# Macaron block on one core (MoE, windowed top-k attention, MoE): the POOL pauses removed and the five interleaving tables replaced

## What is computed

```
x = x + 0.5 * ffn(layernorm(x))
x = x + attn(layernorm(x))
x = x + 0.5 * ffn(layernorm(x))

ffn(x):  n = layernorm(x) * ln_gamma + ln_beta
         gates = softmax over the two largest of softmax(n @ router_w.T)      # 8 experts
         sum over the 2 chosen experts e of gate_e * (silu(n@Wg_e.T) * (n@Wu_e.T)) @ Wd_e.T     # width 384
         + a shared expert of width 128 for every token
attn(x): windows of 128 tokens; q, k, v = x@W.T + b; scores / sqrt(128);
         only the 32 largest scores of each row are kept; softmax; @ v; leaky relu; + x; layernorm * gamma + beta
```

## Time and profile before

| | us |
|---|---|
| median of 3 runs | 647.05 |
| lowest, highest | 643.54, 648.61 |
| the profiled execution | 641.43 |
| its span (first to last instruction) | 639.5 |
| PE busy | 517.6 (81%) |
| POOL busy | 441.3 (69%) |
| DVE busy | 391.3 (61%) |
| ACT busy | 341.0 (53%) |
| mean granted TensorE clock | 0.936 |

### The profile page before, as it was taken

One profiled execution on the slowest core, in us unless ns is written; L12 is line 12 of the kernel. 1 busy time (PEld: TensorE's weight loads), 2 busy tenths in 40 slices (PEclk: granted clock), 3 DMA queues, 4 the chain that ended last, 5 costly groups with the idle time before them and its releaser, 6 DMA issues.

```text
span 639.5 us, 15747 instructions
## 1 busy us (share of the span) xinstructions
PE 517.6 (81%) x3928; PEld 468.7 (73%) x3928; DVE 391.3 (61%) x1785; ACT 341.0 (53%) x816; POOL 441.3 (69%) x806
## 2 busy tenths in 40 slices
PE   2957899779879998987896359887598987999882
PEld 2646797769879898877694348775588977999871
DVE  5586765532255886985797758888567452222454
ACT  3444455364435877745766158673564574455340
POOL 1566878888877457577288815888688888766453
PEclk9995999999989999999899569998799999999897
DMA  6915746566576454764221453531455665676894
GB/s 190 317 45 173 223 164 206 182 211 230 201 256 245 166 191 146 252 215 156 96 88 43 128 175 108 178 113 42 142 196 189 226 213 208 220 282 225 273 316 141
DMA packets 88021, 117.89 MB, mean 184 GB/s; under 512 B 11848, under 2 KB 60880, under 8 KB 87936
## 3 DMA queue, kind: packets, MB, share of 16 engines
q1 hardware_dynamic: 76208, 96.75, 44.8%
q0 software_dynamic: 9312, 19.16, 8.6%
q10 hardware_dynamic: 2416, 0.99, 0.7%
HBM read 26.57 MB, written 26.19 MB: 82 GB/s over the span
## 4 chain that ended last, share of the span: by engine, by line
PE 44%; issue 14%; POOL 12%; DMA 8%; DVE 8%; ACT 7%; SPq 4%; another core or an unknown queue 3%; ACTq 0%; POOLq 0%; DVEq 0%
PE ps_y L732 10%; PE ps_g L718 9%; POOL results L1578 5%; PE ps_h L723 5%; PE ps_u L723 4%; POOL rows L1549 3%; POOL still L1535 3%; DMA xin<-rows 2%; DMA raw_dn<-in_dnw 2%; PE ps_x L712 2%; DVE xres L1308 2%; PE w L676 2%; PE w L630 2%; PE w L660 2%
## 5 line engine op out<-in xcount | busy, mean ns | idle before, releaser
L1578 POOL DMA_INDIRECT results<-raw_gu,idx x163 | 162.5, 997 | 93.4 <-ACT raw_gu L941 50.3
L732 PE MATMUL ps_y<-dn_t,raw_gu 128*128 x978 | 142.5, 283 | 23.4 <-issue 11.1
L1549 POOL DMA_INDIRECT rows<-zz,s_idx x128 | 129.5, 1012 | 32.2 <-issue 17.4
L732 PEld LDWEIGHTS ps_y<-dn_t,raw_gu 128*128 128x128 f32 x978 | 124.3, 194 | 33.3 <-issue 32.6
L718 PE MATMUL ps_g<-x_t,raw_dn 128*128 128x128 f32 x978 | 140.5, 281 | 0.0
L718 PEld LDWEIGHTS ps_g<-x_t,raw_dn 128*128 128x128 f32 x978 | 126.3, 197 | 3.2 <-issue 3.2
L941 ACT COPY raw_gu<-ps_y 128x128 f32<-128x128 f32 x163 | 43.0, 264 | 122.1 <-PE ps_y L732 79.3
L935 ACT ACTIVATE sil<-ps_g 128x384 f32<-128x384 f32 x163 | 80.1, 491 | 48.6 <-PE ps_g L718 30.5
L931 ACT ACTIVATE x_t<-ps_x,bf_c,gf_c 128x128 f32<-128x128 f32 x163 | 75.5, 463 | 44.0 <-PE ps_x L712 32.7
L1381 DVE TENSOR_TENSOR raw_gu<-sil,ps_h 128x384 f32<-128x384 f32 x81 | 44.6, 551 | 82.1 <-PE ps_h L723 33.0
L1535 POOL IOTA still<- 128x200 int32 x291 | 90.7, 312 | 5.6
(11 more groups left out here) (167 smaller groups left out, 761.4 us busy)
## 6 DMA issues: line engine op xcount, KB each, us to landing
raw_dn<-gu_t SPq DMA_DIRECT2D x163, 384.0 KB
xin<-rows SPq DMA_DIRECT2D x163, 64.5 KB
yg<-results SPq DMA_DIRECT2D x15, 512.0 KB
results<-raw_gu,idx POOLq DMA_INDIRECT x163
rows<-pads SPq DMA_DIRECT2D x40, 64.5 KB
rows<-pads SPq DMA_DIRECT2D x5, 451.5 KB
rows<-zz,s_idx POOLq DMA_INDIRECT x128
out<-xres SPq DMA_DIRECT2D x7, 256.0 KB
```

The lines of the kernel that those rows point to most:

```text
L732: t = pe.matmul(ps_y[:, 0, :], h_t[:, k4, c * P:(c + 1) * P], dn[:, bass.ds(off + c * D, D)], start=(c == 0), stop=(c == FC - 1))
L1549: pool.indirect_dma_start(xs, bass.IndirectOffsetOnAxis(s_idx[n][:, c, k:k + 1], 0), zz[n][:, k, c, :], None).then_inc(scat[n], 16)
L1578: pool.indirect_dma_start(yt, bass.IndirectOffsetOnAxis(idx[:, ky:ky + 1], 0), yb[:, ky, :], None).then_inc(yst[ky], 16)
```

## The change

The iota, its tile `still`, its semaphore `rested` and both calls of `apart_in_time` are gone. The five lists of `WEAVE` are replaced: the number of calls of `turn()` and the parts are the same (660 on PE, 497 on ACT, 171 on DVE, 326 on POOL and on SP), their places differ.

```diff
 WEAVE = {
     "sp": """
-        8 3 2 14 2 2 8 5 35 z1 8 50 z1 7 26 z2 58 5 10 2 4 60 4 2 z1 6 z1 2 z1 3 z6""",
+        9 1 17 1 15 z1 8 4 20 12 5 44 3 19 12 z1 33 26 5 2 9 26 38 z1 7 z2 3 z1 2 5 z6""",
...
     "pool": """
-        z20 1 1 z2 1 z1 1 z2 2 2 z2 4 z1 2 z1 2 z1 3 2 z1 1 z1 2 z1 2 1 1 2 z1 2 2 2 2 z1 4 4 4 4 4 3 5 z1 2 4 4 4 2 2 z1 28 18 6 z1 4 z1 4 z1 2 2 z1 6 8 z1 2
-        2 z2 2 1 z2 1 z8 6 4 z1 2 2 2 z2 2 2 z1 6 z1 2 2 1 z5 1 z2 1 5 z1 2 4 2 z1 8 z1 2 2 4 2 z1 1 5 z3 2 6 3 5 z1 4 4""",
+        z19 1 z5 2 z2 5 z1 3 z2 1 z1 5 z1 2 z1 3 1 z3 2 9 4 2 z1 2 2 z2 17 20 z1 3 z2 2 z1 2 1 5 2 2 8 z3 3 3 24 z1 3 1 4 z2 1 z1 8 3 1 3 z4 3 z1 4
+        3 z9 6 z1 8 z1 1 1 z1 2 z2 1 z1 1 z1 2 z3 2 3 5 1 5 z3 2 z1 1 5 2 2 6 z2 2 z2 5 z1 2 13 z2 8 13 3 4 1 23""",
 }
...
-        still = sb("still", [P, 2, 200], I32)
...
-        out_st, spare, rested = sem("out_st"), sem("spare"), sem("rested")
+        out_st, spare = sem("out_st"), sem("spare")
...
-            rests = itertools.count()
-
-            def apart_in_time():
-
-                n = next(rests)
-                if n >= 2:
-                    pool.wait_ge(rested, n - 1)
-                pool.iota(still[:, n % 2, :], pattern=[[1, 200]], base=0, channel_multiplier=0).then_inc(rested, 1)
-
...
                         pool.indirect_dma_start(xs, bass.IndirectOffsetOnAxis(s_idx[n][:, c, k:k + 1], 0),
                                                 zz[n][:, k, c, :], None).then_inc(scat[n], 16)
-                        apart_in_time()
                         turn()
...
                     pool.indirect_dma_start(yt, bass.IndirectOffsetOnAxis(idx[:, ky:ky + 1], 0),
                                             yb[:, ky, :], None).then_inc(yst[ky], 16)
-                    apart_in_time()
```

More of the change, by code:

```diff
@@ L121 @@
+        9 z3 1 2 6 z2 8 z3 2 2 z3 3 3 z2 1 1 z3 2 z1 1 z2 4 z2 1 z1 2 z3 5 z1 1 8 z1 1 z2 1 z4 1 z2 2 1 z21 1 1 1 4 z3 2 z3 4 2 2 7 1 2 z7 1 2 z1 2
+        z4 1 z3 2 3 1 3 1 1 z1 2 z5 1 z2 1 z1 4 3 6 z3 3 z1 7 z3 2 11 3 z2 3 z1 5 50 46 43""",
     "dve": """
-        z51 1 z3 1 z1 1 z6 1 z14 1 z7 1 z2 1 z1 1 z68 2 z9 1 z7 1 z13 1 z9 1 z4 1 z1 1 z10 1 z14 1 z13 2 z4 1 z1 1 z10 1 z10 1 z4 1 z1 1 z5 1 z2 18 z3 1 z5 1
-        z4 1 z7 1 z11 1 1 z1 1 z3 1 z2 1 z3 1 z9 1 z8 1 z11 1 z4 1 z4 1 z3 1 z3 1 z3 1 z7 1 z13 1 1 1 z4 1 z4 1 z7 1 z6 1 z3 1 z9 1 z17 1 z12 1 z3 1 1 z5 1
@@ L124 @@
-        z12 1 z3 1 z3 1 z1 1 z6 1 z5 1 z8 1 z13 1 z28 1 z3 1 z4 1 z5 1 z7 1 z7 1 1 z89 2 z9 1 z32 1 z3 1 z4 1 z4 1 z8 1 z3 1 z4 1 z13 1 z40 1 1 1 z5 1 z6 1
-        z46 1 z17 1 z2 1 z4 1 z10 1 z2 1 1 z23 1 z1 1 z19 1 1 z2 1 z14 4 z25 1 z16 2 z5 2 z2 30 z7 2 z7 2 z7 3 z7 2 z7 1 z7 1 z8""",
+        z68 1 z10 2 z2 1 z3 1 z21 1 z14 1 1 z38 2 z12 2 z11 1 z1 1 z14 1 z1 1 z3 1 z14 1 z8 1 z9 1 z2 2 z3 2 2 z4 1 z3 1 z16 1 1 z3 1 z1 4 3 1 z3 5
+        z9 1 z9 1 z6 3 z7 1 1 z1 1 z10 1 z2 1 z1 1 z14 1 1 z12 1 z7 1 z2 1 z2 1 z2 1 z5 1 z14 1 z5 1 2 z12 1 z3 2 z9 1 z9 1 z1 1 z18 1 z2 1 z8 1 1
@@ L126 @@
+        z4 1 z14 1 z8 2 z15 2 z9 1 z14 2 z28 1 z3 1 z8 1 1 z5 1 z6 1 z10 1 z97 1 z3 1 z3 1 z20 1 z3 1 z9 2 z5 1 z4 1 z19 2 z37 1 z2 1 z12 1 z20 1 1
+        z22 1 z19 1 z2 1 z10 2 z14 2 z16 1 z4 1 1 z6 1 z29 4 z24 1 z2 1 z5 3 z1 4 2 6 z5 1 z1 8 z2 4 z1 2 z2 2 1 z2 2 z5 1 z8 1 z4 1 z3 1 z1 1 1 z2
+        2 z6 2 z15""",
     "pool": """
-        z20 1 1 z2 1 z1 1 z2 2 2 z2 4 z1 2 z1 2 z1 3 2 z1 1 z1 2 z1 2 1 1 2 z1 2 2 2 2 z1 4 4 4 4 4 3 5 z1 2 4 4 4 2 2 z1 28 18 6 z1 4 z1 4 z1 2 2 z1 6 8 z1 2
-        2 z2 2 1 z2 1 z8 6 4 z1 2 2 2 z2 2 2 z1 6 z1 2 2 1 z5 1 z2 1 5 z1 2 4 2 z1 8 z1 2 2 4 2 z1 1 5 z3 2 6 3 5 z1 4 4""",
+        z19 1 z5 2 z2 5 z1 3 z2 1 z1 5 z1 2 z1 3 1 z3 2 9 4 2 z1 2 2 z2 17 20 z1 3 z2 2 z1 2 1 5 2 2 8 z3 3 3 24 z1 3 1 4 z2 1 z1 8 3 1 3 z4 3 z1 4
```

8 lines of the change are left out of this document (3 added, 5 removed).

## The result

The changed kernel takes 711.85 us in the median of 4 runs (711.27 to 715.83), the kernel before 645.29 us (642.73 to 648.61) on the same chip: the ratio is 1.1054, 95% interval 1.1001 to 1.1108. The forecast was 622 us, within 606 to 642. It was wrong in its sign. The profiled execution took 711.72 us, its span 709.8 us at a mean granted clock of 0.886 (before: 639.5 at 0.936).

The account below looks back on a forecast made before the run. The prediction took PE as the main bound, with POOL saturated in two stretches and making PE wait for rows. Terms 8.3 + 6 + 4.5 + 5.9 = 24.7 us off 641.43 gave 616.7, by the ratio 622 us; range 606 to 642.

Parts of the forecast that it names:

- POOL's time: Sign for the whole run: POOL busy near 350 us once the iotas are gone.
- The SP queue's waits behind POOL's number copies: Sign: the SP queue's 68.7 us of waiting for POOL's copies of result numbers falls by half.
- Block 62 and block 148: Sign against the forecast: a new PE wait for rows there would mean step 6's or 15's moved scatters come too late.
- b): Passage between the layers: POOL's scatters finish earlier, so PE's wait for rows shortens; 6 us gained.
- c): Second such wait, at 454 us: POOL's scatter of step 12 comes earlier; 4.5 us gained, bounds 2 and 5.8.
- the slower rival: Back-to-back indirect DMAs hold each other up with 1.49 us records; by the ratio 675 us, chance 0.09.
- What a pause costs: Pricing step over 291 DMAs: 0.25 us saved with a copy between, 0.41 without, 93 us of POOL's time.
- The pitch: Sign: POOL's indirect DMAs follow at 1.00 to 1.16 us, or 1.35 with a copy between.
- a): 64 to 192 us: with POOL freed, PE goes from 86% to 95% busy; 8.3 us gained, bounds 3 to 14.
- d): 480 to 544 us: POOL's time falls by 12 us and PE reaches 95%; 5.9 us gained, bounds 2 and 6.6.
- e): The rest: the new lists alone, at unchanged speeds, are worth 0, with -8 to +8 us.
- The pause covered something: Rival: POOL's descriptor makers stay busy past the DMA record, so pitch stays 1.48; by the ratio 645 us, chance 0.10.

Follow-up runs that it names:

- e2: The changed kernel (new lists) with the pauses put back; 650.11 us, ratio 1.0003 to the kernel before.
- m4: Separate kernel computing nothing of the layers: six phases of back-to-back indirect DMAs beside one engine pair, the last two ACT to DVE and DVE to ACT; latest signal 17.47 us.
- e1: The kernel before with its old lists and the pauses taken out; 675.04 us, ratio 1.0452.
- m2: Separate kernel, layers left out: TensorE streams matmuls beside POOL's DMAs; a round takes 5.02 us with indirect DMAs without pauses, 2.01 with pauses of 480 elements.

## Why the prediction was wrong

**What held.** POOL's time: 353.4 us for about 350. The lists at zero: e2 has 1.0003. The SP queue's waits behind POOL's number copies fell from 68.7 us to half, as said, in the queue's own waits of the kernel after:

```profile
SPq L476 <- POOL idx L1563: 33.8, 12, 10.7
```

Block 62 and block 148 had no new wait for rows; more, PE's three long waits for rows are gone, as b) and c) wanted, but others stand in their place. PE's waits over the whole run:

```profile
PE ps_y L732 <- ACT raw_gu L941: 35.4, 19, 6.0
PE w L610 <- ACT zz L845: 14.4, 2, 10.4
...
PE ps_x L712 <- DMA xin<-rows: 3.6, 4, 1.3
```

The waits for rows are 3.6 us in sum, the longest 1.3. PE waits for what ACT makes of PE's own earlier results instead.

The chain did lose POOL's share. And the indirect DMAs did not become longer: 981 and 976 ns against 997 and 1012. So the price put on the slower rival (1.49 us records) was not paid, nor did what the Trainium skill says on "SBUF — State Buffer", in the box on DVE blocking a DMA, about VectorE keeping POOL from writing descriptors show itself in this kernel. In m4's last two phases, beside a VectorE that never rests, the records do grow, to 4.4 us; why was not tried. The section of that page that the prediction calls "who contends" is headed "Who interferes with whom".

**What failed.** The step is in "What a pause costs": the pause was priced as POOL's time and nothing else. 0.25 and 0.41 us were saved for each of 291 DMAs, and what the gap did for TensorE stood nowhere in the sum, so it was put at nothing. The runs put a value on it: e1 saves 86 us of POOL (441.3 to 355.3 busy) and loses 4.5%, while TensorE's late signals double; m2 isolates it. The direction that the prediction gave to the whole change rests on this step.

The pitch itself was missed too: 1.26 to 1.28 us, for 1.00 to 1.16. The gap with nothing between is 0.30 us, not 0.17; it was extrapolated from the gap behind an iota or a copy. For a DMA without a copy 1.07 was taken and 1.27 came, 0.20 x 128 = 26 us of POOL's time, which POOL had to spare. With a copy between, 1.35 was taken and about 1.32 came (90.15 to 91.47 us in POOL's timeline).

**The terms.**
- *a) 64 to 192 us, 8.3.* It stands on PE going to 95% once POOL is free. POOL became free (69.4 us of 128) and PE stayed at 85%. The reading that took PE's 86% beside a busy POOL for a wait on POOL's queue was at most half of it: 123 us of late signals were there before.
- *b) The passage, 6.* Block 85 begins 131.6 us after block 62, not 122.3 as before. The wait for rows went, and a wait of 10.4 us for ACT's `zz` stands 2.5 us ahead of block 85. The chain that ended last (start us, us, what) goes from the late signal shown above, through routing work of PE and DVE, to this `zz`. Its 7.8 us stand against the 9.3 by which the passage grew:

```profile
357.97 7.83 another core or an unknown queue
365.82 0.28 ACT raw_gu L941
...
402.70 1.57 ACT zz L845 x3
```

- *c) 4.5 and d) 5.9.* The time from block 85 to 102 is 93.9 us and was 81.0, that from 102 to 118 is 68.9 and was 51.2. The second is the stage that lost most, and the clock is 0.74 from 480 to 544 us.
- *e) the lists, 0.* Right with pauses, wrong without. The prediction summed the two edits as if each kept its worth beside the other; 4.5% and 0.0% make 10.5% together.

**The rivals.** "The pause covered something" asked the right question and looked for the cover on POOL alone, in whether its next DMA could start. "Slower" had the right sign by another mechanism, 675 us. The row that should have raised both chances was in the trace: waits of ACT and DVE on TensorE that last over 1 and up to 3.3 us after the matmul's modelled end, 30 of ACT and 28 of DVE, each with an indirect DMA of POOL beside it. The prediction read the waits of PE and none on PE.

## What to carry to other kernels

An instruction whose output nobody reads may be there for its time: before it is taken out, look in the trace at what the other engines do during it, and time the removal alone before anything is planned around it. Where POOL issues indirect DMAs one behind the other while TensorE streams, look for engines that wait on TensorE beyond the end of its matmul (releasers "remote" or "issue" in this profile), and leave about half a microsecond free on POOL between two DMAs in the mean. Two edits that are each harmless or small need not be so together; a list planned for one spacing of transfers is another list under the next.
